# Index tables of a graph kernel: built inside the first preparation block, with half of the tile counts moved to ScalarE

## The chip, the core and the metric

The kernel runs on one core of one Trainium2 chip. The metric is the device time of one execution in microseconds (us), the median of several runs; lower is better.

## The reference, cut to what matters

Four graph layers run one after the other on the same graph: 6,250 nodes with 128 features, 106,250 edges sorted by destination. Each layer gathers rows of nodes by `src` and reduces them by `dst`.

```python
edge_index = jnp.stack([src, dst])
x = _layernorm(x + L0(x, edge_index, node_vec, ...))   # two graph convolutions, segment_max of x[src] / (pos[src] - pos[dst])
x = _layernorm(x + L1(x, ..., src, dst))               # segment_sum of x2[src], in-degree
x = _layernorm(x + L2(x, edge_index))                  # segment_sum of x[dst] by src
x = _layernorm(x + L3(x, edge_index, edge_attr_64, ...))  # GATv2 attention, graph norm
```

Before any layer the kernel builds tables out of `src` and `dst` alone: where each node tile's edges start, which edge tile and node tile each step of a pass works on, and, for the later dense passes, a key and a place for each edge. The change concerns only these tables.

## The kernel before, in words

`build` runs the stages one after the other: `prepare`, `dense_tables`, `max_pass` (gathers of node rows by POOL, one after the other), and then the dense sums and the attention layer. Each stage is a block: every engine runs its own list of instructions, in order, with semaphores between engines, and at the end of a block all engines meet at a barrier, clear the semaphores and meet again.

Edges are taken in tiles of 128, nodes in NT = 49 tiles of 128. An edge array is held as KB = 7 columns of 128 x 128, so one instruction over it has the shape 128x896.

`prepare` (line 102 on) does this:

- SP (`block.sync`, L190 to L215) loads `dst` into `dst_i` and builds the DRAM array `edge_rows` (four rows of indices per edge tile). It then waits for those writes and releases `s_built`, which the gathers of POOL need. At the end it stores the finished tables (L221).
- ACT (`block.scalar`) only issues DMAs: L228 and L230 load `x`, L231 and L232 load node positions, L233 and L234 write `x_sign_pos`, the array that `max_pass` gathers from. After `s_v` has come to V_T it stores the two step tables (L236, L237), reads them back as rows (L239, L240) and stores the signs of `x` (L241).
- DVE (`block.vector`) is one chain: each instruction raises `s_v` and waits for its own increment (`link`). It converts `dst` to float, takes the signs of `x` into `sgn` (which is `y_nodes`, L277), then counts for each of 48 tile borders how many edges lie below it (L282, one instruction of 128x896 for each border). TensorE sums the counts over partitions (L249). Out of them DVE works out `need` (L288 to L295, used by a later pass) and then, column by column, the step tables `T_i` and `t_i` (L296 to L306), which end at V_T.
- POOL then gathers 7 times 128 rows of `edge_rows` (L183). DVE waits for them (`s_rows`), makes the row tables (L309 to L323), copies 21 transposes by TensorE out of PSUM (L329) and ends with L334 and L336.

`dense_tables` (line 1703 on) is the next block. POOL clears buffers (L1737 to L1747), SP issues 12 loads of `src` and `dst` in three alignments and two stores of borders (L1754 to L1772), DVE works out the keys (L1793 to L1813), SP stores them (L1774), TensorE transposes 21 squares and DVE copies them (L1819), and DVE ends with nine instructions on 128x896 (L1822 to L1831) and a copy (L1833).

```python
for T in range(1, NT):
    link(v.tensor_scalar(less[:, :], dst_f[:, :], float(T * P), 0.0, ALU.is_lt, ALU.add,
                         accum_out=cnt[:, T - 1:T]))
```

Of the kernel before, what the change touches and what calls it, by code (L numbers as in the profile page):

```python
# [6 lines left out]
I32 = mybir.dt.int32  # L7
ALU = mybir.AluOpType
ACT = mybir.ActivationFunctionType
# [3 lines left out]
N = 6250  # L13
# [8 lines left out]
P = 128  # L22
# [79 lines left out]
def prepare(nc, g, a):  # L102
# [5 lines left out]
    with ExitStack() as ctx:  # L108
# [44 lines left out]
        ct = g.ct  # L153
        V_X = 5
        V_CNT = V_X + NT - 1
        V_T = V_CNT + 4 + 8 + 5 * KB

        with nc.Block() as block:
            @block.gpsimd
            def _(p):  # L160
# [18 lines left out]

                p.wait_ge(s_v, V_T)  # L180
# [7 lines left out]
            def _(s):  # L188
# [28 lines left out]
                s.wait_ge(s_v, V_T + 13)  # L217
# [8 lines left out]
            def _(s):  # L226
# [7 lines left out]
                s.dma_start(g.xp[0:N, 0:F], a["x"][:, :]).then_inc(s_pos, 16)  # L234
                s.wait_ge(s_v, V_T)
# [4 lines left out]
                s.dma_start(g.t[:, :], g.erow[0:SPX].unsqueeze(0)).then_inc(s_Tl, 16)  # L240
                s.dma_start(g.xp[:, F:2 * F].rearrange("(t p) f -> p t f", p=P), sgn[:, :, :]).then_inc(s_pos, 16)  # L241
# [4 lines left out]
            def _(t):  # L246
# [3 lines left out]
                t.wait_ge(s_v, V_T + 13)  # L250
# [8 lines left out]
            def _(v):  # L259
# [13 lines left out]
                v.wait_ge(s_x, 32)  # L273
# [3 lines left out]
                link(v.tensor_scalar(sgn[:, :, :], g.x[:, :, :], 0.0, 0.5, ALU.is_ge, ALU.subtract))  # L277
# [3 lines left out]
                for T in range(1, NT):  # L281
                    link(v.tensor_scalar(less[:, :], dst_f[:, :], float(T * P), 0.0, ALU.is_lt, ALU.add,  # L282
                                         accum_out=cnt[:, T - 1:T]))
                assert done == V_CNT
                v.wait_ge(s_start, 1)
                link(v.tensor_copy(start_i[:, :], start_ps[:, 0:NT - 1]))
                half = (NT - 1) // 2
# [8 lines left out]
                link(v.tensor_scalar(first_i[:, :], start_i[:, :], 7, None, ALU.arith_shift_right))  # L296
                link(v.tensor_copy(first_f[:, :], first_i[:, :]))
                link(v.tensor_tensor(first_f[:, :], first_f[:, :], tile_no[:, :], ALU.add))
                for b in range(KB):
                    col = slice(b, b + 1)  # L300
                    link(v.tensor_scalar(le[:, :], first_f[:, :], stepno[:, col], 0.0, ALU.is_le, ALU.add,
                                         accum_out=T_f[:, col]))
                    link(v.tensor_copy(T_i[:, col], T_f[:, col]))
                    link(v.tensor_tensor(t_f[:, col], stepno[:, col], T_f[:, col], ALU.subtract))
                    link(v.tensor_scalar(t_f[:, col], t_f[:, col], float(ET - 1), None, ALU.min))
                    link(v.tensor_copy(t_i[:, col], t_f[:, col]))  # L306
                assert done == V_T
# [16 lines left out]
                assert done == V_T + 13  # L324
# [1378 lines left out]
def dense_tables(nc, g, a):  # L1703
# [5 lines left out]
    with ExitStack() as ctx:  # L1709
        m = Memory(nc, ctx)  # L1710
        dst_i, src_i = m.sb("dst_it", [P, KB, P], I32), m.sb("src_it", [P, KB, P], I32)
        next_i = m.sb("next_i", [P, KB], I32)
        high_i = m.sb("high_i", [P, KB, P], I32)
        dst_f, src_f = m.sb("dst_ft", [P, KB, P]), m.sb("src_ft", [P, KB, P])
        far_i, far = m.sb("far_it", [P, KB, P], I32), m.sb("far_ft", [P, KB, P])
        long = m.sb("long_t", [P, 1])
        pad = m.sb("pad_t", [P, KB, P])
        spare = m.sb("spare_t", [P, KB * P], I32)
        spare_row = m.sb("spare_row_t", [P, KB * P], I32)
        mask = m.sb("mask_t", [P, KB * P], I32)  # L1720
        high = m.sb("high_t", [P, KB, P])
        key = m.sb("key_t", [P, KB, P])
        edge = m.sb("edge_t", [P, 2, P])
        first, after = m.sb("first_t", [P, KB]), m.sb("after_t", [P, KB])
        wide = m.sb("wide_t", [P, KB])
        cols_i = m.sb("cols_it", [P, 2, KB * P], I32)
        bad = m.sb("bad_t", [P, 1])
        tr = [m.bank(f"trt{i}") for i in range(2)]
        badp = m.bank("badp")
        s_ini, s_ld = m.sem("s_init_t"), m.sem("s_ldt")  # L1730
        s_v, s_tr, s_cp = m.sem("s_vt"), m.sem("s_trt"), m.sem("s_cpt")
        s_bad, s_out = m.sem("s_badt"), m.sem("s_outt")
        full = ET // P * P
        with nc.Block() as block:
            @block.gpsimd
            def _(p):
                p.memset(dst_i[:, :, :], PAD).then_inc(s_ini, 1)  # L1737
                p.memset(src_i[:, :, :], 0).then_inc(s_ini, 1)
                p.memset(next_i[:, :], PAD).then_inc(s_ini, 1)
                p.memset(far_i[:, :, :], PAD + 1).then_inc(s_ini, 1)  # L1740
                p.memset(edge[:, :, :], -1.0).then_inc(s_ini, 1)
                p.memset(spare_row[:, :], NT * P).then_inc(s_ini, 1)
                p.iota(spare[:, :], [[P, KB * P]], base=0, channel_multiplier=1).then_inc(s_ini, 1)
                p.memset(g.earlier[:, :], EARLIER).then_inc(s_ini, 1)
                p.wait_ge(s_ini, 8)

# [1342 lines left out]
```

## Time and profile before

| | |
|---|---|
| median of 3 runs | 5190.69 us (5190.12 to 5192.56) |
| the profiled execution's own time | 5189.41 us |
| its span in the profile | 5187.6 us |
| busy share of the span: PE, DVE, ACT, POOL | 73%, 65%, 28%, 56% |
| start of `prepare` to the last instruction of its block's chain | 0 to 135.2 us |
| first instruction of `dense_tables` to that of `max_pass` (POOL) | 139.24 to 183.42 us |
| from there to the end | 5004 us |

The times in the rows are microseconds from the start of the span. Engine names ending in q (ACTq, SPq) stand for DMAs that the engine's own instruction stream issues; the duration is the time of the issue, not of the transfer. "idle before" is time in which the engine did nothing ahead of the instruction, and what ended it.

### The profile page before, as it was taken

Reading aid. Unit: us, or ns where it says so; the run is one execution under the profiler, and the core shown is the slowest. Engines: PE = TensorE matmul, PEld = TensorE weight load, DVE = VectorE, ACT = ScalarE, POOL = GpSimd, SP = SyncE. Lnnn points to the kernel's source line nnn. Section 1 sums busy time; section 2 is a strip of 40 time slices with the busy share of each in tenths; the row PEclk is TensorE's granted clock in tenths of the full one; section 3 lists DMA queues with packets and bytes.
Section 4 is the critical chain, followed back from the end, with each engine's and each line's share of the span. In section 5 each row is a group of like instructions: output and inputs, shape, how many; then the busy total and the mean of one; then the engine's idle time right before and its main releaser. Section 6 shows DMA issues by size and latency. Waiting matters only on the chain. (4 is left out here: it accounts for less than half of the span.)

```text
span 5187.6 us, 87634 instructions
## 1 busy us (share of the span) xinstructions
PE 3774.7 (73%) x17756; PEld 2581.4 (50%) x17757; DVE 3380.9 (65%) x10123; ACT 1428.3 (28%) x3423; POOL 2918.1 (56%) x2917
## 2 busy tenths in 40 slices
PE   0377777777677777389979988889899883555553
PEld 0266666666434444145546655555555552444442
DVE  5688888888798888343242234445444446788878
ACT  0255555555344434200000012222222221000012
POOL 1477777777367777777400007777777770333334
PEclk9955555665688888689989995555555555999996
DMA  5577777777532232088966636666666663655540
GB/s 104 154 249 250 248 247 248 247 249 254 164 97 87 87 92 91 10 183 199 180 182 205 204 113 171 177 174 179 174 176 177 175 168 59 174 143 142 143 106 25
DMA packets 1057791, 843.64 MB, mean 163 GB/s; under 512 B 546821, under 2 KB 952950, under 8 KB 1044160
## 3 DMA queue, kind: packets, MB, share of 16 engines
q1 hardware_dynamic: 785772, 597.52, 39.1%
q0 software_dynamic: 98096, 176.73, 13.3%
q10 hardware_dynamic: 173844, 68.53, 5.5%
q8 instruction: 26, 0.43, 0.0%
q14 instruction: 53, 0.43, 0.0%
HBM read 601.40 MB, written 167.28 MB: 148 GB/s over the span
## 5 line engine op out<-in xcount | busy, mean ns | idle before, releaser
L2303 POOL DMA_INDIRECT ring<-xl_rows,idx x896 | 895.2, 999 | 847.8 <-DVE idx L2382 575.0
L413 POOL DMA_INDIRECT ringa<-x_sign_pos,idxa x880 | 865.3, 983 | 301.6 <-issue 295.5
L965 POOL DMA_INDIRECT edge_counts<-edge_cnt,places x832 | 827.2, 994 | 359.9 <-issue 272.1
L2375 PE MATMUL zps<-We,eaT 64*128 64x128 f32 x1792 | 712.0, 499 | 0.0
L2649 PE MATMUL ops<-val,hot 128*128 128x200 f32 x1792 | 369.1, 350 | 273.5 <-DVE out L2668 243.1
L2373 PE MATMUL zps<-xr,hotT 128*128 x2688 | 455.2, 302 | 145.1 <-ACT hotT L2355 89.8
L2405 DVE TENSOR_TENSOR z<-zps,ring 128x512 f32<-128x512 f32 x224 | 154.9, 691 | 605.1 <-PE zps L2375 510.0
L2375 PEld LDWEIGHTS zps<-We,eaT 64*128 64x128 f32 x1792 | 448.6, 310 | 163.3 <-issue 145.7
L2616 POOL TENSOR_TENSOR val<-rows,val 128x512 f32<-128x512 f32 x224 | 235.0, 1050 | 508.4 <-ACT val L2635 377.6
L498 PE MATMUL sela<-hota,endsa 128*128 128x128 f32 x1760 | 399.3, 398 | 132.1 <-ACT endsa L439 117.6
L1890 PE MATMUL pss<-x3s,mats 128*128 128x385 bf16 x2401 | 403.4, 330 | 100.9 <-DMA mats<-edge_counts 95.9
L2649 PEld LDWEIGHTS ops<-val,hot 128*128 128x128 f32 x1792 | 301.2, 193 | 341.3 <-DVE out L2668 308.0
L2033 PE MATMUL psd<-x3d,matd 128*128 128x384 bf16 x2401 | 391.7, 327 | 35.3 <-DVE x3d L2064 35.3
L498 PEld LDWEIGHTS sela<-hota,endsa 128*128 128x128 f32 x1760 | 342.3, 290 | 149.9 <-issue 102.9
L2373 PEld LDWEIGHTS zps<-xr,hotT 128*128 128x128 bf16 x2688 | 225.3, 121 | 361.6 <-issue 354.9
L2351 ACT ACTIVATE apartT<-dstb,minus_p 128x512 f32<-128x512 f32 x224 | 161.7, 722 | 869.6 <-DMA dstb<-dst_in_tile 866.0
L2668 DVE TENSOR_TENSOR out<-out,ops 128x200 f32 x896 | 321.5, 359 | 115.5 <-PE ops L2649 17.6
L1890 PEld LDWEIGHTS pss<-x3s,mats 128*128 128x128 bf16 x2401 | 235.2, 98 | 269.2 <-DMA mats<-edge_counts 83.8
L1240 DVE SCALAR_TENSOR_TENSOR equalb<-keyb,key_cols,earlier 128x256 f32<-128x256 f32 x850 | 359.9, 481 | 5.9 <-issue 3.3
L506 PE MATMUL msgTa<-ident,msga 128*128 128x128 f32 x880 | 241.2, 428 | 153.3 <-DVE msga L578 150.8
L2033 PEld LDWEIGHTS psd<-x3d,matd 128*128 128x128 bf16 x2401 | 235.3, 98 | 191.7 <-DVE x3d L2064 35.7
L570 DVE TENSOR_TENSOR acc<-acc,sela 128x128 f32 x880 | 251.9, 286 | 117.5 <-issue 16.4
(359 smaller groups left out, 5945.3 us busy)
## 6 DMA issues: line engine op xcount, KB each, us to landing
edge_counts<-zeroa SPq DMA_DIRECT2D x55, 1568.0 KB
matd<-edge_counts SPq DMA_DIRECT2D x12, 6272.0 KB
keyb<-edge_keys SPq DMA_DIRECT2D x50, 1216.0 KB
dstb<-dst_in_tile SPq DMA_DIRECT2D x112, 512.0 KB
xl_of_steps<-ring SPq DMA_DIRECT2D x224, 256.0 KB
rows<-xl_of_steps SPq DMA_DIRECT2D x224, 256.0 KB
reseta<-resets SPq DMA_DIRECT2D x110, 512.0 KB
dstba<-dst_in_tile_bf ACTq DMA_DIRECT2D x112, 256.0 KB
```

The lines of the kernel that those rows point to most:

```text
L413: p.indirect_dma_start(out=ring[:, k, :], out_offset=None, in_=table, in_offset=bass.IndirectOffsetOnAxis(ap=idx[:, k:k + 1], axis=0)).the ...
L498: ins = t.matmul(sel[q % 2][:, k * P:(k + 1) * P], ends[:, q % 2, k, :], hot[:, q, k, :], start=True, stop=True)
L570: v.tensor_tensor(to, to, sel[q % 2][:, k * P:(k + 1) * P], ALU.add).then_inc(s_acc, 1)
L965: p.indirect_dma_start(out=g.M.rearrange("d s -> (d s)").unsqueeze(1), out_offset=bass.IndirectOffsetOnAxis(ap=g.place[:, c:c + 1], axis=0 ...
L1240: v.scalar_tensor_tensor(out=equal[:, k % 4, :], in0=keyb[:, i, k * P + HALF:k * P + HALF + WIN], scalar=g.keycol[:, bass.ds(tile, 1)], in ...
L1890: ins = t.matmul(ps[b * WC + k][:, 0:3 * F + 1], mat[:, b, T, k * P:(k + 1) * P], x3[:, T, 0:3 * F + 1], start=T == 0, stop=T == NT - 1)
L2033: ins = t.matmul(ps[k][:, 0:3 * F], mat[:, b, T, k * P:(k + 1) * P], x3[:, T, :, :].rearrange("p i f -> p (i f)"), start=T == 0, stop=T == ...
L2303: p.indirect_dma_start(out=ring[:, c, k, :], out_offset=None, in_=g.xl_rows[0:N, :], in_offset=bass.IndirectOffsetOnAxis(ap=idx[:, q * GS ...
L2373: t.matmul(zk, hotT[:, b, k * P:(k + 1) * P], g.xr3[:, bass.ds(T[k] * (3 * F) + i * F, F)], start=i == 0, stop=False)
L2375: ins = t.matmul(zk, eaT[:, c, k, :], g.We[:, :], start=False, stop=True)
L2649: ins = t.matmul(ops[q % 2][k // 2][:, (k % 2) * FX:(k % 2 + 1) * FX], hot[:, c, k, :], val[:, c, k, :], start=True, stop=True)
L2668: v.tensor_tensor(to, to, ops[q % 2][k // 2][:, (k % 2) * FX:(k % 2 + 1) * FX], ALU.add).then_inc(s_out, 1)
```

## The change

1. `dense_tables` is no longer a block of its own. It allocates its buffers in `prepare` (five of them now lie in `g.acc`, which is not used yet at that point) and returns five pieces of program, which `prepare` puts into the lists of its engines: POOL's clearing ahead of POOL's wait for V_T, SP's loads and its store of the keys ahead of SP's final stores, TensorE's transposes ahead of the others, and DVE's whole table chain between the step tables and the wait for the gathered rows.
2. Of the 48 counts DVE makes 24. ACT makes the other 24, behind its first six DMAs, as the sum of sign(border - 0.5 - dst) over 896 elements; DVE turns the sums into counts with one instruction, behind a wait for ACT (`s_sign`).
3. DVE no longer waits for `x` (`s_x`) at its start. The signs of `x` and `need` are worked out behind the step tables, not ahead of them. ACT's store of the signs waits for V_T + 1.
4. The four small instructions on each column of the step tables become four on all seven columns at once.

```diff
+        half_ps = (NT - 1) // 2
+        bound, sums = m.sb("bound_of_tile", [P, P]), m.sb("sums_of_sign", [P, NT - 1 - half_ps])
+        sign = g.acc[:, 0:2 * KB * P].rearrange("p (i e) -> p i e", i=2)
...
+        tables_pool, tables_sync, tables_out, tables_tensor, tables_vector = dense_tables(g, a, m)
...
+                tables_pool(p)
                 p.wait_ge(s_v, V_T)
                 p.wait_ge(s_built, 16 * 7)
...
                 s.wait_ge(s_padded, 32 + 48)
                 s.sem_inc(s_built, 16)
-                s.wait_ge(s_v, V_T + 13)
+                tables_sync(s)
+                tables_out(s)
+                s.wait_ge(s_v, V_N + 13)
...
                 s.dma_start(g.xp[0:N, 0:F], a["x"][:, :]).then_inc(s_pos, 16)
+                for i, T in enumerate(range(half_ps + 1, NT)):
+                    s.wait_ge(s_v, V_X)
+                    wait(s, s_sign, i - 1)
+                    s.activation(sign[:, i % 2, :], dst_f[:, :], ACT.Sign, scale=-1.0, bias=bound[:, T - 1:T],
+                                 accum_out=sums[:, i:i + 1]).then_inc(s_sign, 1)
                 s.wait_ge(s_v, V_T)
...
+                s.wait_ge(s_v, V_T + 1)
                 s.dma_start(g.xp[:, F:2 * F].rearrange("(t p) f -> p t f", p=P), sgn[:, :, :]).then_inc(s_pos, 16)
...
-                t.wait_ge(s_v, V_T + 13)
+                tables_tensor(t)
+                t.wait_ge(s_v, V_N + 13)
...
                 v.wait_ge(s_init, 12)
-                v.wait_ge(s_x, 32)
...
-                link(v.tensor_scalar(sgn[:, :, :], g.x[:, :, :], 0.0, 0.5, ALU.is_ge, ALU.subtract))
+                link(v.tensor_scalar(bound[:, :], g.iota_n[:, :], float(P), P - 0.5, ALU.mult, ALU.add))
                 link(v.memset(less[:, :], 0.0))
                 assert done == V_X
-                for T in range(1, NT):
+                for T in range(1, half_ps + 1):
                     link(v.tensor_scalar(less[:, :], dst_f[:, :], float(T * P), 0.0, ALU.is_lt, ALU.add,
                                          accum_out=cnt[:, T - 1:T]))
+                v.wait_ge(s_sign, NT - 1 - half_ps)
+                link(v.tensor_scalar(cnt[:, half_ps:], sums[:, :], 0.5, KB * P / 2, ALU.mult, ALU.add))
                 assert done == V_CNT
...
                 assert done == V_T
+                v.wait_ge(s_x, 32)
+                link(v.tensor_scalar(sgn[:, :, :], g.x[:, :, :], 0.0, 0.5, ALU.is_ge, ALU.subtract))
...
+                assert done == V_N
+                tables_vector(v)
                 v.wait_ge(s_rows, 16 * KB)
...
                 prepare(nc, g, a)
-                dense_tables(nc, g, a)
```

Three places show how the instructions now stand. The first is ACT in `prepare`. Before, behind the write of `x_sign_pos` by L234:

```order
L233 DMA x_sign_pos<-in_node_vec 6250x1
L234 DMA x_sign_pos<-in_x 6250x128
L236 DMA node_tile_of_step<-T_i 128x7x1 [waits s_v]
L237 DMA edge_tile_of_step<-t_i 128x7x1
L239 DMA T<-node_tile_of_step 1x896 [waits s_T]
```

and now:

```order
L242 DMA x_sign_pos<-in_node_vec 6250x1
L243 DMA x_sign_pos<-in_x 6250x128
L247 ACT_TABLE_LOAD
L247 ACTIVATE acc,sums_of_sign<-dst_f,bound_of_tile 128x896 [waits s_v] x2
L247 ACTIVATE acc,sums_of_sign<-dst_f,bound_of_tile 128x896 [waits s_sign,s_v] x22
L250 DMA node_tile_of_step<-T_i 128x7x1 [waits s_v]
```

The table load and 24 activations stand between the same DMAs. The table load that stood in `max_pass` (L453) is gone from there.

The second place is DVE, from the counts to the wait for the gathered rows, in the changed kernel:

```order
L297 TENSOR_SCALAR less,cnt<-dst_f 128x896 [waits s_v] x24
L300 TENSOR_SCALAR cnt<-sums_of_sign 128x24 [waits s_sign,s_v]
L303 CAST start_i<-start_ps 128x48 [waits s_start,s_v]
...
L309 TENSOR_SCALAR le,T_f<-first_f,stepno 128x48 [waits s_v] x7
L311 CAST T_i<-T_f 128x7 [waits s_v]
L312 TENSOR_TENSOR t_f<-stepno,T_f 128x7 [waits s_v]
L313 TENSOR_SCALAR t_f<-t_f 128x7 [waits s_v]
L314 CAST t_i<-t_f 128x7 [waits s_v]
L317 TENSOR_SCALAR y_nodes<-x_nodes 128x6400 [waits s_x,s_v]
...
L1806 CAST acc<-dst_it 128x896 [waits s_init_t,s_ldt,s_v]
...
L1846 COPY bad<-badp 128x1 [waits s_badt,s_vt]
L330 CAST rows_f<-rows 128x3584 [waits s_rows]
```

The whole table chain (L1806 to L1846) now stands in the same list ahead of the first instruction that needs the gathered rows.

The third place is SP, behind the writes of `edge_rows`, in the changed kernel:

```order
L219 DMA edge_rows<-in_dst 9x1
L1768 DMA dst_it<-in_dst 128x6x128 [waits s_padded,s_init_t]
...
L1786 DMA edge_keys<-edge_t 1x128
L1789 DMA edge_keys<-key_t 128x7x128 [waits s_vt]
L230 DMA resets<-flag 128x7x128 [waits s_v,s_outt]
L230 DMA dst_in_tile<-drel_r 128x7x128
```

The 12 loads, the two stores of borders and the store of the keys stand ahead of the four final stores.

## Rows read from the trace of the kernel before

**Rows 1.** Timeline, last early DMA issues of ACT and SP (start us, us, engine, line, operation)
```profile
35.29 21.11 ACTq L234 DMA_DIRECT2D x_sign_pos<-in_x  x1
...
55.69 2.17 SPq L212 DMA_DIRECT2D edge_rows<-in_dst  x3
```

**Rows 2.** Timeline of ACT in the pass behind: a DMA issue between two activations
```profile
193.51 0.33 ACTq L444 DMA_DIRECT2D dstba<-dst_in_tile_bf  x1
193.89 0.63 ACT L458 ACTIVATE hotTa<-aparta 128x512 bf16<-128x512 f32 x1 [0.41 <-ACT aparta L453]
```

**Rows 3.** Timeline of DVE in `prepare`, start to step tables
```profile
26.33 0.29 DVE L274 TENSOR_SCALAR valid<-ones,iota_p 128x128 f32<-128x128 f32 x1 [26.21 <-DMA x_nodes<-in_x]
...
27.57 3.50 DVE L277 TENSOR_SCALAR y_nodes<-x_nodes 128x6400 f32<-128x6400 f32 x1
...
32.16 1.08 DVE L282 TENSOR_SCALAR_CACHE_REDUCE less<-dst_f 128x896 f32<-128x896 f32 x1
...
87.21 0.21 DVE L286 CAST start_i<-start_ps 128x48 int32<-128x48 f32 x1 [0.88 <-PE start_ps L249]
87.45 0.18 DVE L288 TENSOR_SCALAR need_i<-start_ps 128x24 int32<-128x24 f32 x1
...
89.09 0.19 DVE L296 TENSOR_SCALAR first_i<-start_i 128x48 int32<-128x48 int32 x1
...
89.78 0.26 DVE L301 TENSOR_SCALAR_CACHE_REDUCE le<-first_f,stepno 128x48 f32<-128x48 f32 x1
...
90.09 0.15 DVE L303 CAST T_i<-T_f 128x1 int32<-128x1 f32 x1
...
90.84 0.26 DVE L301 TENSOR_SCALAR_CACHE_REDUCE le<-first_f,stepno 128x48 f32<-128x48 f32 x1
```

**Rows 4.** Timeline, the first gather and the instruction that waits for the last
```profile
97.48 1.13 POOL L183 DMA_INDIRECT rows<-edge_rows,t_i  x1 [88.53 <-DVE t_i L306]
...
115.10 2.03 DVE L309 CAST rows_f<-rows 128x3584 f32<-128x3584 int32 x1 [17.91 <-DMA rows<-edge_rows,t_i]
```

**Rows 5.** Timeline, end of `prepare`: sign store, last table store, DVE's end, next block
```profile
109.65 0.39 ACTq L241 DMA_DIRECT2D x_sign_pos<-y_nodes  x1
...
129.06 5.48 SPq L221 DMA_DIRECT2D src_rows<-rows_f  x1
...
134.60 0.63 DVE L336 TENSOR_SCALAR dst_of_ends<-dst_of_ends 128x896 f32<-128x896 f32 x1
139.24 0.84 POOL L1737 MEMSET dst_it<- 128x896 int32 x1 [33.12 <-POOLq L78]
```

**Rows 6.** Timeline of `dense_tables`: DVE's first and last, and the next block
```profile
152.84 0.63 DVE L1793 CAST dst_ft<-dst_it 128x896 f32<-128x896 int32 x1 [17.61 <-DMA far_it<-in_dst]
...
182.57 0.16 DVE L1833 COPY bad<-badp 128x1 f32<-128x1 f32 x1
183.42 5.32 POOL L401 MEMSET zeroa<- 128x6272 bf16 x1 [39.06 <-POOLq L78]
```

**Rows 7.** Waits of SP's queue, 0 to 184 us (engine line <- waited for: us, times, longest)
```profile
SPq L215 <- DMA edge_rows<-in_dst: 8.6, 1, 8.6
...
SPq L158 <- DMA src_rows<-rows_f: 3.8, 1, 3.8
```

**Rows 8.** Groups of ACT by line and shape (busy us, mean ns)
```profile
L2351 ACT ACTIVATE apartT<-dstb,minus_p 128x512 f32<-128x512 f32 x224 | 161.7, 722 | 869.6 <-DMA dstb<-dst_in_tile 866.0
...
L2895 ACT ACTIVATE partn<-x_nodes,negn 128x128 f32<-128x128 f32 x50 | 19.4, 390 | 25.2 <-DVE negn L2815 25.2
...
L453 ACT ACT_TABLE_LOAD x1 | 1.3, 1283 | 178.1 <-DMA dstba<-dst_in_tile_bf 178.1
```

**Rows 9.** Timeline of ACT: activations with an accumulated sum, one after the other
```profile
5140.07 0.39 ACT L2895 ACTIVATE partn<-x_nodes,negn 128x128 f32<-128x128 f32 x1
...
5140.45 0.38 ACT L2895 ACTIVATE partn<-x_nodes,negn 128x128 f32<-128x128 f32 x1
```

**Rows 10.** A stretch of 4 us: PE, PEld, DVE, ACT, POOL busy (x), PEclk, DMA share, GB/s
```profile
128.00:132.00 4.00, 3.15 (x10) 1.65 (x10) 2.52 (x10) 0.00 (x0) 0.00 (x0) 1.00 1.22 164
```

More of the change, by code:

```diff
@@ L153, in prepare @@
         ct = g.ct
+        half_ps = (NT - 1) // 2
+        bound, sums = m.sb("bound_of_tile", [P, P]), m.sb("sums_of_sign", [P, NT - 1 - half_ps])
+        sign = g.acc[:, 0:2 * KB * P].rearrange("p (i e) -> p i e", i=2)
+        s_sign = m.sem("s_sign")
         V_X = 5
-        V_CNT = V_X + NT - 1
-        V_T = V_CNT + 4 + 8 + 5 * KB
+        V_CNT = V_X + half_ps + 1
+        V_T = V_CNT + 4 + KB + 4
+        V_N = V_T + 9
+        tables_pool, tables_sync, tables_out, tables_tensor, tables_vector = dense_tables(g, a, m)
         with nc.Block() as block:
@@ L286, in _ @@
                 link(v.tensor_copy(start_i[:, :], start_ps[:, 0:NT - 1]))
+                link(v.tensor_scalar(first_i[:, :], start_i[:, :], 7, None, ALU.arith_shift_right))
+                link(v.tensor_copy(first_f[:, :], first_i[:, :]))
+                link(v.tensor_tensor(first_f[:, :], first_f[:, :], tile_no[:, :], ALU.add))
+                for b in range(KB):
+                    col = slice(b, b + 1)
+                    link(v.tensor_scalar(le[:, :], first_f[:, :], stepno[:, col], 0.0, ALU.is_le, ALU.add,
+                                         accum_out=T_f[:, col]))
+                link(v.tensor_copy(T_i[:, :], T_f[:, :]))
+                link(v.tensor_tensor(t_f[:, :], stepno[:, :], T_f[:, :], ALU.subtract))
+                link(v.tensor_scalar(t_f[:, :], t_f[:, :], float(ET - 1), None, ALU.min))
+                link(v.tensor_copy(t_i[:, :], t_f[:, :]))
+                assert done == V_T
+                v.wait_ge(s_x, 32)
+                link(v.tensor_scalar(sgn[:, :, :], g.x[:, :, :], 0.0, 0.5, ALU.is_ge, ALU.subtract))
                 half = (NT - 1) // 2
@@ L295, in _ @@
                 link(v.tensor_scalar(g.need[:, :, 1], need_odd[:, :], 16 * PUT, None, ALU.mult))
[L296 to L307, printed above, removed]
+                assert done == V_N
+                tables_vector(v)
                 v.wait_ge(s_rows, 16 * KB)
@@ L323, in _ @@
                 link(v.tensor_tensor(g.pos3[:, :, 2], pos_rest[:, :], g.pos3[:, :, 1], ALU.subtract))
-                assert done == V_T + 13
+                assert done == V_N + 13
                 i = 0
```

235 lines of the change are left out of this document (114 added, 121 removed).

## The prediction

> **What bounds the kernel now.** I read the page first: it gives the 5187.6 us span and shows that the stages are separated by barriers, so an early stage shortened by a microsecond should shorten the whole by a microsecond. The change touches only what lies ahead of the first instruction of `max_pass`, which POOL starts at 183.42 [rows 6]. So the question is what that start waits for. The timeline of the first 184 us answers it, read backward: `dense_tables` runs from 139.24 [rows 5] to 183.42 [rows 6], 44.2 us, in which DVE first sits idle until 152.84 for loads and then works for 29.9 us, until 182.7. Ahead of it `prepare` is one chain on DVE. The reader is to see its sections: DVE starts at 26.33, when `x` has landed; 48 counts run from 32.16 to 86.33 (87.21 less 0.88 of idle time), 1.128 us each; the step tables are ready at 97.2 [rows 3]; then DVE waits 17.9 us for POOL's gathers, until 115.10 [rows 4]; then it works until 135.2, and the block ends at 139.24 [rows 5]. The last 4 us are not DVE's: SP waited 3.8 us for the store of `src_rows` to land [rows 7].
>
> **When the counts are complete.** DVE's half is 24 x 1.128 = 27.1 us. DVE no longer waits for `x`; even from the old start at 26.33, with some 3 us of small work, it is through by 57. ACT's half decides, and it can't start early. Its activations stand in program order behind its DMA issues, and the last of these occupies ACT until 35.29 + 21.11 = 56.4 [rows 1]. That such an issue does hold up the activations behind it is seen in the pass behind: the issue of 0.33 us ends at 193.84 and the activation starts at 193.89 [rows 2]. Then come a table load, 1.28 us [rows 8], and 24 signs on 896 elements. No such instruction is in the trace. An activation with a summed output on 128 elements repeats every 0.38 us, its read of the sum included [rows 9]; between 128 and 512 elements the duration grows from 390 to 722 ns [rows 8], 0.865 ns an element; 768 more elements are 0.66 us. I take 1.04 us, 25.1 us for 24. From below, none takes less than 0.72 us, the 512-element row: 17.3 us. From above, if all of the 0.38 us grew with the elements, 2.66 us: 63.8 us. I choose the middle value since two rows of different length show a fixed part. ACT is done at 56.4 + 1.3 + 25.1 = 82.8, and DVE's scaling of the sums, one small instruction, ends at **83.0**, against 86.33 before. So halving the counts gains only **3.3 us**, not 27: DVE will stand idle from before 57 to 83.
>
> **From the counts to the step tables.** Before, 86.33 to 97.2, 10.9 us. What remains: 0.88 for TensorE's sum, 0.24 for the copy, 0.69 for three instructions (89.09 to 89.78), 7 x 0.31 for the compare of each column, and four instructions on seven columns at about the 0.75 us that four now take on one column (90.09 to 90.84), say 0.8 [rows 3]. Together 4.8 us. The step tables are ready at **87.8**, 9.4 us earlier than before. `need` (1.64 us, 87.45 to 89.09) and the signs of `x` (3.5 us and 0.25 of idle time) only move behind [rows 3].
>
> **From there to the gathered rows.** POOL gathers at once, and the last row comes 17.9 us later, at 105.7 [rows 4]. `edge_rows` is ready by then: SP's last issue ends at 57.86 [rows 1], and the writes land 8.6 us later, at 66.5 [rows 7]. DVE does meanwhile 3.75 + 1.64 + 29.9 = 35.3 us of work, until **123.1**. The 17.9 us of waiting are covered by it, 17.4 us to spare. The table loads must have landed at 93.2. SP issues them from 66.5, behind its wait; all of it, clearing included, took 13.6 us (139.24 to 152.84) [rows 5, 6], so about 80. POOL's clearing starts right behind its first fills, tens of microseconds ahead of its wait for 87.8, and costs nothing. TensorE's 21 transposes are the same ones. SP's store of the keys is issued inside DVE's table chain, before 123.1, and behind it on SP stand only the final stores, which are due at about 132 (123.1 and the 8.8 us of row tables, 115.10 to 123.9). ACT's store of the signs waits for V_T + 1, true 3.75 us behind V_T, while ACT gets there only 12.4 us behind it (109.65 less 97.2) [rows 5]; no wait there.
>
> **The end of the block.** From DVE's first use of the rows to the next block it took 139.24 - 115.10 = 24.1 us. Of that DVE's own work is 20.1 (to 135.23) [rows 4, 5], and the end of a block costs 0.7 us where nothing else is late (182.73 to 183.42) [rows 6]. The rest is SP's wait for its stores, one of whose issues alone took 5.48 us [rows 5] at a DMA share above 1 [rows 10]: ACT's store of the signs, issued at 109.65, was still under way. In the new order that store is issued at 100.2 and SP's stores at 132, so they no longer meet, and the stores should land while DVE still copies transposes. I take 21.1, between 20.8 (no wait at all) and 24.1 (as before). `max_pass` then starts at 123.1 + 21.1 = **144.2** in place of 183.42.
>
> **Sum.** -9.4 (step tables) - 17.9 (gather wait) + 35.3 (signs, `need`, tables) - 3.0 (end of block) - 44.2 (block gone) = **-39.2 us**. The profiled execution took 5189.4, which gives 5150.2; the median of the runs is 1.3 above it, so I forecast **5151.5**. The table load that leaves `max_pass` is worth between nothing and its 1.28 us [rows 8]; I take nothing, since ACT's first activation there waits for DVE, which first clears the accumulator. About 0.2%, 10 us, is what a measurement of this kernel can tell from no change.
>
> **A rule that speaks against the change.** DVE now works through the 17.9 us in which POOL writes the descriptors of the gathers; before it was idle there [rows 4]. The trace has no row of the two together, so from rows: DVE could at worst keep POOL off until its tables are done, and the gathers would start at 123.1, landing at 141.0; or POOL could hold DVE up for 7 gathers of at most 1.13 us, 7.9 us. I add nothing: the first needs a delay of over 17.4 us to be felt, and DVE's long instructions leave gaps. The Trainium skill, "SBUF — State Buffer", section "Who interferes with whom", says that a DVE instruction in a two-port mode and a GpSimd instruction exclude each other for its whole length, and names casts and `tensor_scalar` as able to enter such a mode, and that gathers issued by POOL starve for descriptors then. By it the sum would move by something between nothing and the first of these cases; no row here shows it.
>
> **Rivals.**
> - *The gathers starve.* DVE's chain wins every time, and the rows come 17.9 us behind 123.1. For it: the overlap is new. Against: most of the chain is many short instructions, the one of 3.5 us the longest [rows 3]. Time: 5151.5 + 17.9 = 5169. Chance 4%.
> - *ACT does not wait for its own DMA issues*, or they end far earlier. Signs would start at about 30 and end by 56; the step tables come by 62, the gather waits for `edge_rows` at 66.5, the tables for their loads at about 77 to 80. DVE reaches the rows at about 108.5, `max_pass` starts at 129.6, 54 us earlier: 5137. Against: [rows 1, 2]. Chance 4%.
> - *Slower: the signs are expensive.* ACT's signs are now the only thing ahead of the step tables, and every microsecond of one sign costs 24. From 1.04 + 39.2 / 24 = 2.68 us a sign the change gains nothing, and just this is the upper bound of 2.66 (all of the time of rows 9 in proportion). At 3.1 us it is 5151.5 + 24 x 2.06 = 5201. Against: rows of 512 elements at 0.72 us [rows 8]. Chance 3%.
> - *The gain is not carried to the end*: a later stage absorbs it in part, as where a DMA-bound stage starts against other traffic. Against: everything behind starts from a barrier with idle queues, as before. Time some 5160 to 5175. Chance 5%.
> - The forecast as worked out: 84%.
>
> **How the numbers follow.** The forecast's own range: signs between 0.72 and 1.3 us (-7.7 to +6), end of block -0.3 to +3, DVE held up by POOL 0 to +7.9, the median of a few runs +-1.5. These don't add up all at once: 5144 to 5162 leaves out the two ends of cases that are 16% together. Faster by over 0.2% (below 5180.3) is the forecast and three rivals, 0.95; within 0.2% the signs near 2.66 us, 0.02; slower 0.03.
>
> **What would show it.** Right: ACT's first sign at 57 to 58; 24 signs, 1.0 to 1.1 us apart; DVE idle for over 25 us ahead of its scaling instruction, released by ACT; POOL's first gather near 88; no wait of DVE at the cast of `rows_f`, which starts near 123; that of the first table instruction (L1806) not on a DMA; short SP issues at the end, and POOL's first memset of `max_pass` near 144. From there to the end 5004 us as before. Wrong: a first sign long before 56; a DVE wait on the gather; DVE instructions of 0.63 us grown longer beside the gathers; or a different length of the stages behind 144.

## The result and the profile after

The changed kernel took **5155.55 us** (median of 7 runs, 5150.16 to 5179.78) against 5197.79 us for the kernel before (7 runs, 5190.12 to 5206.64). The ratio over all runs is 0.9933, 95% interval 0.9912 to 0.9954 (that of the two medians alone is 0.9919). The seven runs of the changed kernel form two groups, four at 5150.2 to 5155.6 and three at 5170.3 to 5179.8. The profiled one (5171.5, span 5169.5) is of the second, outside the forecast's range. In the order of the record the three long runs came first, where the kernel before took 5190.1 to 5192.6 us, and the four short ones behind, where it took 5197.8 to 5206.6: by medians the gain is 19 us in the first part and 47 us in the second.

**The preparation.** ACT in the changed kernel, its last early DMA issues and the first signs (timeline; start us, us, engine, line, operation):

```profile
33.64 1.68 ACTq L242 DMA_DIRECT2D x_sign_pos<-in_node_vec  x1
35.36 19.83 ACTq L243 DMA_DIRECT2D x_sign_pos<-in_x  x1
55.22 1.28 ACT L247 ACT_TABLE_LOAD   x1 [46.67 <-issue]
56.51 1.04 ACT L247 ACTIVATE acc<-dst_f,bound_of_tile 128x896 f32<-128x896 f32 x1
57.46 0.19 ACT L247 ACTIVATION_READ_ACCUMULATOR acc<-dst_f,bound_of_tile 128x1 f32 x1
57.55 1.02 ACT L247 ACTIVATE acc<-dst_f,bound_of_tile 128x896 f32<-128x896 f32 x1
```

This answers to [rows 1]. ACT was idle for 46.67 us with no semaphore to blame; its own DMA issues held it until 55.2. DVE meanwhile finished its half and waited for ACT (timeline):

```profile
51.92 1.09 DVE L297 TENSOR_SCALAR_CACHE_REDUCE less<-dst_f 128x896 f32<-128x896 f32 x1
...
81.33 0.18 DVE L300 TENSOR_SCALAR cnt<-sums_of_sign 128x24 f32<-128x24 f32 x1 [28.31 <-ACT acc L247]
82.39 0.21 DVE L303 CAST start_i<-start_ps 128x48 int32<-128x48 f32 x1 [0.89 <-PE start_ps L264]
...
86.08 0.17 DVE L314 CAST t_i<-t_f 128x7 int32<-128x7 f32 x1
86.28 3.49 DVE L317 TENSOR_SCALAR y_nodes<-x_nodes 128x6400 f32<-128x6400 f32 x1
...
91.65 0.83 DVE L1806 CAST acc<-dst_it 128x896 f32<-128x896 int32 x1
...
121.57 0.16 DVE L1846 COPY bad<-badp 128x1 f32<-128x1 f32 x1
121.64 2.02 DVE L330 CAST rows_f<-rows 128x3584 f32<-128x3584 int32 x1
```

The last row answers to [rows 4]: the 17.91 us wait is gone, and DVE takes up the rows at once. The issue of the last store is short now, 1.38 us against 5.48 in [rows 5] (SP and POOL, timeline):

```profile
132.74 1.38 SPq L230 DMA_DIRECT2D src_rows<-rows_f  x1
...
142.83 5.33 POOL L422 MEMSET zeroa<- 128x6272 bf16 x1 [43.51 <-POOLq L78]
```

| | forecast | measured |
|---|---|---|
| first sign; spacing | 57.7; 1.04 us | 56.5; 1.03 us |
| counts complete | 83.0 | 81.5 |
| step tables | 87.8 | 86.25 |
| DVE takes up the rows | 123.1 | 121.6 |
| start of `max_pass` (183.42 before) | 144.2 | 142.8 |
| from there to the end of the span (5004.2 before) | 5004 | **5026.7** |

So 40.6 us were gained ahead of `max_pass` and 22.5 us lost behind it, in stages whose code the change doesn't touch but for one table load.

**The later stages**, from their first and last instructions, in two profiles of the kernel before and three of the changed one. Those named before_again, after_again and after_third are of the runs below:

| us | before | before_again | after | after_again | after_third |
|---|---|---|---|---|---|
| start of `max_pass` to that of `first_layer` | 1222.7 | 1222.9 | 1227.5 | 1230.2 | 1227.1 |
| `first_layer` | 795.8 | 795.8 | 797.5 | 794.4 | 794.0 |
| `dense_sum` | 441.0 | 457.0 | 458.4 | 457.5 | 444.2 |
| end of `dense_sum` to the end of the span | 2544.1 | 2551.3 | 2542.7 | 2548.2 | 2544.0 |
| start of `max_pass` to the end of the span | 5004.2 | 5027.6 | 5026.7 | 5030.9 | 5009.9 |

`dense_sum` has two lengths, and each kernel shows both. PE's waits within it for the transposing loads of the count matrix tell them apart (engine line waited for: us in total, times, longest). Before, and the same kernel again:

```profile
PE pss L1890 <- DMA mats<-edge_counts: 95.9, 4, 83.3
```
```profile
PE pss L1890 <- DMA mats<-edge_counts: 110.6, 5, 83.4
```

After, and the same changed kernel again (after_third):

```profile
PE pss L1905 <- DMA mats<-edge_counts: 111.8, 5, 82.3
```
```profile
PE pss L1905 <- DMA mats<-edge_counts: 98.3, 4, 83.3
```

It is the total that differs, 12 to 16 us, not the number of waits: over the 14 profiles at usual speed the short form (441 to 445 us) has 94 to 99 us of waiting in 3 to 5 waits, the long form (455 to 458 us) 109 to 112 us in 4 or 5. In the kernel before the difference stands in one place. SP issues 25 such loads, most of them in 11.3 to 13.6 us; the 21st takes longer in both forms, and by 13 us more in the long one (timeline of SP, before and before_again):

```profile
2538.89 24.15 SPq L1880 DMA_TRANSPOSE mats<-edge_counts  x1
```
```profile
2543.49 37.55 SPq L1880 DMA_TRANSPOSE mats<-edge_counts  x1
```

The changed kernel shows the same: 39.9 us in "after", 26.5 in after_third. PE then waits 25 to 27 us for this load in the long form and 11 to 15 in the short one.

Two other differences are smaller. `max_pass` is longer by 4 to 7.5 us in all three profiles of the changed kernel. And what stands behind `dense_sum` varies by 8.6 us among the five, by 7.2 us between two executions of the unchanged kernel.

### The profile page after: what moved, and what is told of

It is laid out like the page before. It is cut to its first block and busy times, and to the rows that moved or that the text cites. A ratio compares the mean times of both kernels' runs of the same rounds, so it can differ in the third digit from the quotient of the medians.

```text
span 5169.5 us, 87611 instructions
## 1 busy us (share of the span) xinstructions
PE 3785.0 (73%) x17756; PEld 2587.4 (50%) x17757; DVE 3343.0 (65%) x10053; ACT 1454.5 (28%) x3471; POOL 2921.0 (57%) x2917
## 3 DMA queue, kind: packets, MB, share of 16 engines
q1 hardware_dynamic: 785772, 597.52, 39.8%
```

## The experiments

Each kernel is compared with the kernel before on the same chip; the first four share one chip, the second four and the last four another, and the three between them a third. "Start" is the start of `max_pass`, "rest" the time from there to the end of the span. "Turn" is the mean time from one 16 gathers of `max_pass` to the next on POOL, over 53 of its 55 turns (all but the first and the last); gaps are POOL's idle times of over 0.5 us between the 880 gathers.

### The two kernels again, and each half of the change alone

**before_again** and **after_again** are the two kernels without an edit.

> The kernel before, unchanged, with a profile of its own. Preparation and tables should end at 183.4 us as before (within 1 us). The question is the length of everything behind, 5004 us in the first profile. Theory 'spread': the later stages differ from one execution to the next by 10 us and more whatever stands ahead of them; then this profile may give 4995 to 5030 us, with max_pass (1195 us) or dense_sum (441 us) off by several us. Theory 'the change lengthens the later stages': this gives 5004 us within 3 us again. Time equal to the kernel before within 0.1%.

Measured: 5202.52 us (12 runs, 5196.77 to 5216.08), ratio 0.9989 (0.9975 to 1.0002), start 186.4, rest 5027.6. The unchanged kernel has a rest 23 us longer, like "after", in its profiled run of 5215.8: 16.0 us of it are `dense_sum`, 7.2 us lie behind it. The start, expected within 1 us of 183.4, came 3 us later.

> The changed kernel, unchanged. max_pass starts at 142.8 us within 1 us. Behind it the first profile took 5026.7 us, 22.5 us more than before, of which dense_sum 17.8 and max_pass 7.4. Theory 'spread': these do not come again together; the time is 39 to 42 us below the kernel before measured beside it (ratio 0.9920 to 0.9925). Theory 'the change lengthens the later stages': 5022 to 5030 us again, ratio 0.996 to 0.997.

Measured: 5166.75 us (6 runs, 5158.68 to 5179.51), ratio 0.992 (0.990 to 0.994), start 146.6, rest 5030.9, `dense_sum` 457.5. Here too the runs fall into two groups, three near 5159 and three at 5173.7 to 5179.5. The start is 39.8 us before that of before_again, but 3.8 us behind that of "after": on this chip ACT's write of 6250 rows held it until 58.96 and the first sign came at 60.28. The profiled run has the long `dense_sum` and the longer `max_pass` again, as the theory of lengthened stages says; the ratio over the six runs is that of the theory of spread.

**all_on_dve**: the tables stay inside `prepare`, DVE makes all 48 counts.

```diff
-                for i, T in enumerate(range(half_ps + 1, NT)):
...
-                for T in range(1, half_ps + 1):
+                for T in range(1, NT):
...
-                v.wait_ge(s_sign, NT - 1 - half_ps)
-                link(v.tensor_scalar(cnt[:, half_ps:], sums[:, :], 0.5, KB * P / 2, ALU.mult, ALU.add))
```

> The changed kernel with all 48 counts on VectorE again (no signs on ScalarE); the tables stay inside the preparation. Theory 'ScalarE is held by its DMA issues until 55 us, so the split of the counts gains nothing': VectorE counts from 25.95 to 25.95 + 48 x 1.128 = 80.1 us, 1.4 us ahead of the 81.5 of the changed kernel, and max_pass starts near 141.5; time equal to the changed kernel within 2 us. Rival 'the split pays its 24 counts': max_pass starts at 142.8 + 27 = 170 us and the time is 27 us above the changed kernel.

Measured: 5161.71 us (5158.41 to 5162.95), ratio 0.9913 (0.9896 to 0.993), start 149.2, rest 5007.2. The intervals of this and of after_again overlap: without ACT's half nothing measurable is lost. The start was expected near 141.5. DVE's counts did end at 80.1, as expected (in after_again ACT's last sign ended at 85.0), but DVE then had to wait for the table loads (timeline of DVE):

```profile
98.22 0.63 DVE L1799 CAST acc<-dst_it 128x896 f32<-128x896 int32 x1 [8.03 <-DMA far_it<-in_dst]
```

**counts_only**: the split counts stay, the tables go back into a block of their own, behind `prepare`.

```diff
-                tables_vector(v)
...
+                tables_block(nc, g, a)
```

> The changed kernel with the tables in a block of their own again behind the preparation; counts split, small instructions merged, signs of x behind the step tables. Theory 'the gain is the removed block and the covered gather wait': step tables at 86.3, DVE waits for the gathers until about 104 us (18 less 5.4 us of other work), then 24.1 us to the end of the block and 44.2 us of tables: max_pass starts at about 172.5 us, 11 us ahead of the kernel before, and the time is 9 to 12 us below it. Rival 'the reordering of the counts carries the gain': 25 us or more below it.

Measured: 5206.27 us (12 runs, 5195.82 to 5215.27), ratio 1.000 (0.9988 to 1.0013), start 179.1 where 172.5 was expected, rest 5024.6. The start is only 7.3 us before that of before_again, and in the median nothing of it is left. DVE waits for the gathered rows again (timeline):

```profile
107.95 2.03 DVE L324 CAST rows_f<-rows 128x3584 f32<-128x3584 int32 x1 [14.15 <-DMA rows<-edge_rows,t_i]
```

Here ACT's store of the signs, issued at 102.4, and SP's last stores meet as in the kernel before: SP's last issue takes 6.44 us.

So in the medians the whole gain comes with the tables inside `prepare`; no run moves the tables and changes nothing else. The 9.4 us that the forecast gives the counts and step tables together is a gain of the start alone, and it comes mostly with the shorter step tables and the missing wait for `x`, which all_on_dve has too (its step tables are ready at 84.8).

### What holds ACT, and what comes next

**signs_early**: ACT's loop of signs stands ahead of its two loads of positions and its two writes of `x_sign_pos`, not behind them.

```diff
                 for i, T in enumerate(range(half_ps + 1, NT)):
...
+                s.dma_start(pos[:, 0:NT - 1], a["node_vec"][0:(NT - 1) * P].rearrange("(t p) -> p t", p=P)).then_inc(s_nodes, 16)
...
+                s.dma_start(g.xp[0:N, 0:F], a["x"][:, :]).then_inc(s_pos, 16)
```

> The changed kernel with ScalarE's 24 signs ahead of its position loads and of the writes of x_sign_pos, in place of behind them. Theory 'ScalarE's own DMA issues hold its signs': the first sign comes at 27 us in place of 56.5 to 60.3, both halves of the counts end at 53, the step tables at 58 (86 to 90 in the changed kernel), and VectorE then waits for the table loads, which SP issues only at 64.5 and which land by 85 to 98: table chain from there, max_pass at 135 to 149 us, so that most of the 28 us is lost to that wait and the time is 0 to 8 us below the changed kernel. Rival 'the signs are late for another reason (a wait for dst, a slow activation)': the first sign stays behind 50 us.

Measured: **5145.81 us** (5136.81 to 5153.31), ratio 0.9898 (0.988 to 0.9916), start 129.4, earlier than the 135 to 149 expected. ACT's timeline shows the cause removed, and where it went:

```profile
25.72 1.04 ACT L243 ACTIVATE acc<-dst_f,bound_of_tile 128x896 f32<-128x896 f32 x1 [4.82 <-DVE less L293]
```
```profile
54.37 15.89 ACTq L248 DMA_DIRECT2D x_sign_pos<-in_x  x1
70.30 22.26 ACTq L250 DMA_DIRECT2D node_tile_of_step<-T_i  x1
92.60 1.76 ACTq L251 DMA_DIRECT2D edge_tile_of_step<-t_i  x1
...
105.76 0.39 ACTq L256 DMA_DIRECT2D x_sign_pos<-y_nodes  x1
```

The first sign comes at 25.7, not 56.5, and the step tables at 57.7. But the write of 6250 rows now comes later, and the small store behind it (0.41 us in the kernel "after") takes ACT 22.26 us. The store of the signs is issued at 105.8 and meets SP's last stores. The next two fences are the waits of SP's queue and a stretch of 10 us (PE, PEld, DVE, ACT, POOL busy, PEclk, DMA share, GB/s):

```profile
SPq L164 <- DMA src_rows<-rows_f: 9.5, 1, 9.5
```
```profile
118.00:128.00 10.00, 0.00 (x0) 0.00 (x0) 0.26 (x1) 0.00 (x0) 0.00 (x0) 1.00 1.08 235
```

DVE is done at 118.3, and the block waits for 11 us more with every engine idle and the DMA share at 1.08.

**both_early**: signs_early, and SP's table loads stand ahead of its writes of `edge_rows`.

```diff
+                tables_sync(s)
...
-                tables_sync(s)
```

> signs_early, and SP's 12 table loads ahead of its writes of edge_rows. Theory: step tables at 58, no wait of VectorE for loads, table chain 63 to 93; the gathers wait for edge_rows, some 8 us later than before (72 to 75), and bring their rows by 94; max_pass starts at 115 to 118 us if the writes of x_sign_pos, issued until about 88 and followed by the 3.3 MB of signs from about 100, are done by then, and at 120 to 128 us if they are not. Time 20 to 31 us below the changed kernel (ratio to the kernel before 0.986 to 0.989). Rival 'the preparation is bound by its DMA traffic, not by VectorE's chain': max_pass stays behind 135 us.

Measured: 5147.31 us (5143.47 to 5152.28), ratio 0.9905 (0.9889 to 0.9922), start 130.5. DVE was done at 113.0, 5.3 us before signs_early, and the start came no earlier, where 115 to 128 was expected. ACT's small store was held for 24.42 us:

```profile
69.97 24.42 ACTq L250 DMA_DIRECT2D node_tile_of_step<-T_i  x1
```

From 113.0 to 129 no engine computed, while the DMA share was 0.87 to 1.22. DVE no longer bounds this block. The transfers do.

**dve_loads_early**: all_on_dve with the table loads early.

> all_on_dve (48 counts on VectorE) with SP's 12 table loads ahead of its writes of edge_rows. In all_on_dve VectorE was ready for the table chain at 90.2 us and began it at 98.2. Theory 'the 8 us are the late table loads': the chain begins at 90 to 91, max_pass at 141 to 142 us, 7 to 8 us ahead of all_on_dve. Rival 'those 8 us come from elsewhere': 149 us again.

Measured: 5154.16 us (5152.18 to 5156.56), ratio 0.9919 (0.9902 to 0.9935), start 141.2, rest 5009.0. The wait of 8 us is gone. That the early loads removed it isn't shown: all_on_dve ran on another chip, and signs_unused below, on this chip with the loads late, has no such wait either and starts at the same time.

**signs_unused**: 48 counts on DVE, and ACT's 24 signs are made too, but nothing uses their sums.

```diff
-                for T in range(1, half_ps + 1):
+                for T in range(1, NT):
...
-                v.wait_ge(s_sign, NT - 1 - half_ps)
-                link(v.tensor_scalar(cnt[:, half_ps:], sums[:, :], 0.5, KB * P / 2, ALU.mult, ALU.add))
```

> all_on_dve with the 24 signs on ScalarE kept, but used by nobody (VectorE counts all 48 borders). One question: the length of max_pass, whose turn of 16 gathers takes 21.17 us (mean of 53) in the kernel before, 21.22 in all_on_dve and 21.29 to 21.31 in the three kernels with signs on ScalarE. Theory 'the signs on ScalarE (its instruction stream, the table load moved ahead) lengthen the turns': 21.29 to 21.31 us, max_pass 1202 to 1204 us. Rival 'something else in the split counts, or chance': 21.17 to 21.23 us.

Measured: one run, 5151.72 us, start 141.4, rest 5008.4, turn 21.21 us. The start is 1.4 us before that of "after" and 1.9 us before that of after_third, which ran on this chip; the same kernel's start moved by up to 3.8 us between chips. With ACT held until 55.7, DVE alone is as fast as the two. And ACT's list isn't what makes `max_pass` longer, since the turn is short here with the signs in place.

### The longer `max_pass`, on a slow chip

By then every profile of a kernel with 24 counts on DVE had some 80 gaps and a turn of 21.29 to 21.31 us, and every one with 48 had about 45 gaps and 21.16 to 21.23. The theory: what counts is where `max_pass` stands in DVE's list of instructions. **after_filler** is the changed kernel with 48 small instructions at DVE's start, beside its 23 us wait for `dst`:

```diff
-        V_X = 5
+        filler = m.sb("filler", [P, 1])
+        V_X = 5 + 48
...
+                for _ in range(48):
+                    link(v.memset(filler[:, :], 0.0))
```

> The changed kernel with 48 memsets of 128x1 more on VectorE, at the very start, while it waits for dst. So far a turn of 16 gathers in max_pass took 21.16 to 21.23 us in the five kernels in which VectorE makes 48 counts (two instructions each in the profile) and 21.29 to 21.31 in the five in which it makes 24, whether or not ScalarE computes signs. Theory 'the place of max_pass in VectorE's list of instructions decides': 48 short instructions in place of the 48 that left bring the turn back to 21.16 to 21.23 and max_pass to 1195 to 1200 us; the start of max_pass stays at 142.8 to 146.6. Rival 'something else in the split counts': 21.29 to 21.31 and 1202 to 1205 us.

**signs_store_sp** is both_early with the store of the signs issued by SP:

```diff
+                s.wait_ge(s_v, V_T + 1)
+                s.dma_start(g.xp[:, F:2 * F].rearrange("(t p) f -> p t f", p=P), sgn[:, :, :]).then_inc(s_pos, 16)
```

> both_early with the store of the signs of x (3.2 MB) issued by SP behind its writes of edge_rows, in place of by ACT as its last. In both_early VectorE was through at 113.0 us and max_pass started only at 130.5, since ACT issued that store at 108.9, behind its own x_sign_pos writes and the step tables. Theory 'that store ends last': it is issued near 62, lands by 110, and max_pass starts at 114 to 118 us, 12 to 16 us earlier; time 12 to 16 us below both_early. Rival 'the DMA traffic as a whole binds': max_pass at 125 us or later, since the same bytes move in another order.

**sp_filler** is both of these edits together.

> signs_store_sp with the 48 memsets of after_filler. If the place in VectorE's list decides, 5 to 8 us below signs_store_sp, all of it in max_pass (turn 21.16 to 21.23 against 21.29 to 21.31). If not, the same as signs_store_sp.

Measured: 6548.13, 6524.98 and 6535.05 us, against 6584.48 (17 runs) for the kernel before on this chip; ratios 0.9948 (0.9928 to 0.9967), 0.9915 (0.9889 to 0.994) and 0.9935 (0.9917 to 0.9953). This chip was 27% slower than the others, with the kernel before and with the changed one with the filler (5156.5 us further below). Here POOL waits in `max_pass` for buffers, 620 gathers in the stretch from 200 to 1300 us in place of 827 to 832 at the usual speed (group of sp_filler, by line and shape):

```profile
L437 POOL DMA_INDIRECT ringa<-x_sign_pos,idxa x620 | 605.1, 976 | 495.1 <-DVE msga L602 267.2 <-issue 227.3 <-DVE idxa L571 0.6
```

A turn took over 28 us in all three, so these runs could not settle the question of 0.1 us a turn, and the ratios don't order the three kernels: `max_pass` was 5.3 us shorter in sp_filler than in signs_store_sp, as the theory says, but the median was 10 us longer. One thing stands: moving the sign store to SP (issued at 62.15) did not free the end. ACT was held by its store for longer still, and the start was at 140.0, where 114 to 118 was expected, although DVE was done at 113.3:

```profile
87.34 33.04 ACTq L252 DMA_DIRECT2D node_tile_of_step<-T_i  x1
120.42 6.50 ACTq L253 DMA_DIRECT2D edge_tile_of_step<-t_i  x1
137.22 0.24 ACTq L255 DMA_DIRECT2D T<-node_tile_of_step  x1
```

### The filler on a chip of usual speed

**after_third** is the changed kernel, **after_filler_b** is after_filler, **early_filler** is signs_early with the filler, **signs_early_b** is signs_early.

> The changed kernel once more, unchanged, as the partner of after_filler_b on one chip. Both theories expect the turn of 16 gathers in max_pass at 21.29 to 21.31 us, as in the two earlier profiles of it, against 21.16 to 21.18 in the kernel before, and the start of max_pass at 142 to 147 us. dense_sum takes either about 442 or about 456 us.

> The changed kernel with 48 linked memsets of 128x1 at the start of VectorE's list, beside its wait for dst. Theory A (the longer turn of max_pass comes from where max_pass stands in VectorE's list of instructions, which became 24 counts shorter): the turn falls to 21.16 to 21.23 us and max_pass is 4 to 8 us shorter than in after_third. Theory B (it comes from where the buffers lie or from ACT's list): the turn stays at 21.29 to 21.31 us, and max_pass is the same within 1 us.

> signs_early with the same 48 memsets. Theory A: the start of max_pass stays at 129 to 130 us, the turn falls to 21.16 to 21.23 us, and the time is 4 to 8 us below signs_early_b. Theory B: the same as signs_early_b within 2 us.

> signs_early once more, unchanged, as the partner of early_filler on one chip: the start of max_pass at 129 to 130 us, the turn at 21.29 to 21.31 us, the time 15 to 22 us below after_third.

| | us (range) | ratio (95%) | start | rest | turn | gaps | `dense_sum` |
|---|---|---|---|---|---|---|---|
| after_third | 5157.53 (5150.99 to 5162.32) | 0.9924 (0.991 to 0.9937) | 143.3 | 5009.9 | 21.28 | 80 | 444.2 |
| after_filler_b | 5156.53 (5148.23 to 5160.48) | 0.9919 (0.9905 to 0.9932) | 143.4 | 5005.9 | 21.25 | 46 | 441.4 |
| early_filler | **5142.40** (5141.91 to 5143.40) | 0.9893 (0.9878 to 0.9908) | 133.2 | 5008.2 | 21.22 | 45 | 442.0 |
| signs_early_b | 5145.16 (5141.57 to 5150.16) | 0.9898 (0.9883 to 0.9913) | 131.1 | 5014.6 | 21.30 | 82 | 442.5 |

The filler does change the pattern in `max_pass`: gaps fall from 80 and 82 to 46 and 45, the number of the kernels with 48 counts. POOL's unexplained waits there, from 200 to 1300 us, in after_third and in after_filler_b (us, times, longest):

```profile
POOL ringa L434 <- issue: 285.6, 823, 2.1
```
```profile
POOL ringa L437 <- issue: 280.3, 817, 2.1
```

The kernel before has 279.1 there and "after" 283.8. But the size came out differently in the two pairs: from `max_pass` to `first_layer` early_filler was 6.2 us shorter than signs_early_b, after_filler_b only 1.2 us shorter than after_third, where theory A expected 4 to 8, and its turn stayed 0.02 us above the band. In the medians of the runs, 1.0 and 2.8 us, neither can be told from nothing. Over the 14 profiles at usual speed the two groups don't overlap: the seven with 24 counts and no filler have 76 to 82 gaps and 1227.1 to 1230.2 us from `max_pass` to `first_layer`, the other seven 43 to 46 gaps and 1222.6 to 1225.9 us. So it is shown that instructions ahead of a loop in DVE's list change the rhythm of the loop. What about them does it is not (the filler also adds a buffer of 128x1 and raises the semaphore values by 48), nor that it makes all of the 4 to 7.5 us of the changed kernel: after_filler_b has few gaps and was still 3.2 us longer than the kernel before. The starts expected for early_filler and signs_early_b, 129 to 130, came at 133.2 and 131.1, and signs_early_b was 12.4 us below after_third where 15 to 22 was expected. early_filler is the fastest kernel of the study, level with signs_early_b, and both are ahead of the changed kernel on the same chip.

## Why the prediction was right and where it failed

- **When the counts are complete** was right in mechanism and size. ACT can't start its signs before its own DMA issues are done; 56.5 against 57.7, 1.03 us a sign against 1.04 (the middle value, worked out from two rows of different length [rows 8, 9]). The row that was to show that an issue holds up activations [rows 2] didn't: it names ACT's own `aparta` as what ended the 0.41 us of idle time. signs_early shows the cause by taking it away. The rival that ACT is not held falls with it. Its start of `max_pass`, 129.6, against 129.4 in signs_early, is luck: it had DVE at the rows at 108.5 and 21.1 us from there, and signs_early took 98.1 and 31.3.
- **From the counts to the step tables** was 4.75 us against 4.8 (81.5 to 86.25).
- **From there to the gathered rows**: the wait of 17.9 us was covered, as forecast. What the rule against the change forecasts does happen, but the spare time hides it. The first gather took 4.24 us, beside DVE's 3.49 us instruction, against 1.13 in [rows 4]; the other six took 0.94 to 1.48 us. In dve_loads_early, where the gather began 0.7 us later, it took 3.53 us, and in both it ended 1.0 us behind the DVE instruction. In signs_store_sp, where that instruction was over before the gather began, it took 1.13 us again. "After", then signs_store_sp:

```profile
86.54 4.24 POOL L190 DMA_INDIRECT rows<-edge_rows,t_i  x1 [72.52 <-DVE t_i L314]
91.08 0.94 POOL L190 DMA_INDIRECT rows<-edge_rows,t_i  x1 [0.30 <-issue]
```
```profile
62.97 1.13 POOL L190 DMA_INDIRECT rows<-edge_rows,t_i  x1 [48.95 <-DVE need_i L324]
```

  By the Trainium skill, "SBUF — State Buffer", section "Who interferes with whom", a DVE instruction in a two-port mode that was issued first locks POOL out for its whole length; the trace agrees with the length (the mode itself is in no row). From the step tables to the end of the last gather it was 13.1 us in place of 8.9: 4.1 of the 17.4 us to spare, 3.1 of them in the first gather. In the other direction DVE lost 0.4 us in two instructions (0.83 in place of 0.63 us at L1806, 0.39 in place of 0.18 at L322, which is 0.18 again in signs_store_sp), not up to 7.9.
- **The end of the block**: 21.2 us against 21.1. The reading that the sign store and SP's last stores meet held: in "after" the last issue takes 1.38 us and the DMA share was 0.00 ahead of those stores; in counts_only, where they meet, it takes 6.44. SP's wait for the last store is still 3.7 us, but it ends before DVE does. Where the early signs push ACT's stores late the meeting comes back, and the wait is 9.5 us.
- **The sum up to `max_pass`**: -40.6 against -39.2.
- **The step that failed** is "From there to the end 5004 us as before", with the term that stands for it in the range, "the median of a few runs +-1.5". The rest took 5026.7 us in "after". By 17.4 us that is `dense_sum`, which takes 441 to 445 or 455 to 458 us, whatever the kernel: before_again has the long form without the change, after_third the short one with it. 4.8 us more are `max_pass`. The one trace of before had the short form, and its three runs, 2.4 us apart, hid the spread; over 7 runs it was 16.5 us. With the short form the time is in the forecast's range (after_third: 5155.2 in the profiled run, 5157.5 in the median), though its rest is 5.7 us longer than 5004.2.
- **The median of 5155.6 us is in the range in part by luck.** Three of the seven runs are outside of it, at 5170.3 and more; with one more of these among the seven the median would be too. And the kernel before, whose 5190.7 us the sum starts from, took 5197.8 over its seven runs.
- **The gain is not carried to the end**, the rival with 5%, named the time of two of the three longer runs (5160 to 5175) but a wrong reason. No later stage absorbs the gain; one stage is long or short in both kernels, and `max_pass` is 4 to 7.5 us longer through a thing that no row of before shows, its rhythm under another list of instructions. This term the forecast lacked altogether.
- **Split counts**: the forecast gave them 3.3 us. They are worth nothing measurable in the order in which the change puts them (signs_unused and dve_loads_early start 1.9 to 2.1 us before after_third on the same chip, all_on_dve 2.6 us behind after_again). Moved ahead of ACT's DMA issues they give 12 us of start (131.1 against 143.3 on one chip).

What stays open: why the issue of the 21st transposing load of `dense_sum` takes 13 us more in some executions (only one execution of each run is profiled, so that the groups of 5150 to 5160 and 5170 to 5180 are its two forms is argued from their distance, not shown), and how much of `max_pass` the instruction list accounts for.

## What to carry to other kernels

A DMA issue can hold the engine that issues it, with all compute behind it (the write of 6250 rows held ACT for 8.8 to 30.1 us in these runs): before giving such an engine work, look at when its last issue ends, and put the work ahead. Then follow what the moved issues now collide with; here the bound went from DVE to the transfers at once. And a forecast from one trace carries the spread of stages that it doesn't touch: read the same stage in two executions before setting the range.

## What the runs showed of the hardware

- A small DMA issue behind a large one is held too: the store of 128x7 steps took ACT 0.41 us when it came 31 us after the end of the issue of the 6250-row write ("after"), and 19.79 to 33.04 us when it came right behind it (early_filler, signs_early, both_early, signs_store_sp).
- A gather issued 0.26 us behind the start of a 3.49 us DVE instruction took 4.24 us, and 1.13 us with that instruction out of its way.
- 48 memsets ahead of a loop, hidden beside a wait, change the number of gaps in a loop that begins over 100 us behind them (80 to 46, and 82 to 45).
- One transposing load among 25 like it held SP for 23.5 to 28.1 us in some executions and for 37.4 to 39.9 us in others, whatever the kernel.
- One chip was 27% slower than the others (6584.48 against some 5200 us for the same kernel). From after_filler_b to after_filler, the same kernel, the time from `max_pass` to `first_layer` grew from 1226 to 1615 us and `dense_sum` from 441 to 726. All of the latter lies in one stretch of after_filler: TensorE was busy from 2960 to 2970 us (55 matmuls, granted clock 0.89), and then, up to about 3290 us, the clock was at 0.50, the lower level of 1.2 GHz, and TensorE made 36 matmuls in 100 us, 2.8 us apart (3000 to 3200 us), waiting for nothing that the profile shows; the DMA share was 0.16 and 0.02. From 3320 us on it made 608 in 100 us again at 1.00. Why is open.
- The activation table load took 1.28 us, and the first sign began 0.01 us after it.
